# Normalising ahead of a gate, weight places read three chunks sooner, transposes one chunk later, in a vision tower with routed experts

## The reference, cut to what matters

```python
h = patch_embedding(x)                                  # 64 images, 37 tokens each, 256 wide
h = h + attention_0(layernorm(h))
x = layernorm(h)                                        # this stage holds the change
out = expert(x, sg, su, sd)                             # shared expert: silu(x sg') * (x su') sd', width 704
probs = softmax(x @ wr.T + rb)                          # 7 routed experts, the best 2 of each token
scores, idx = top_k(probs, 2); scores = scores / scores.sum(-1)
w = sum(scores[..., None] * one_hot(idx, 7), axis=-2)
h = h + out + sum(w[..., e] * expert(x, rg[e], ru[e], rd[e]) for e in range(7))
h = h + attention_1(layernorm(h))
h = h + gated_ffn_1(layernorm(h))
```

## Time and profile before

| | |
|---|---|
| median of 3 runs | 1051.48 us (1050.4 to 1051.73) |
| the profiled execution, its own time | 1051.63 us |
| its span, first to last instruction | 1049.8 us |
| mean granted clock of PE | 0.975 |
| shared expert with routing | 237 to 401 us of the span |
| routed experts | 401 to 712 us |
| busy: PE, DVE, ACT, POOL | 971.6, 709.0, 660.5, 359.1 us |

### The profile page before, as it was taken

How to read it: one execution, slowest core, us unless ns; L and a number is a source line. 1 busy time by engine, 2 the same in 40 slices (tenths; PEclk the granted TensorE clock), 3 DMA queues, 4 the chain that set the end, 5 groups by cost and what they waited for, 6 DMA issues and landing times.

```text
span 1049.8 us, 29183 instructions
## 1 busy us (share of the span) xinstructions
PE 971.6 (93%) x10745; PEld 892.2 (85%) x10746; DVE 709.0 (68%) x1393; ACT 660.5 (63%) x1206; POOL 359.1 (34%) x285
## 2 busy tenths in 40 slices
PE   4979999989999987999999999997899999799998
PEld 4967888868888886999999999996678888699998
DVE  3536677675556566899999999992566777655443
ACT  3337677855465635687777777772567678555652
POOL 0253454465665650111111111113545554611210
PEclk9999999989999998999999999999889999999999
DMA  6720000009211135111111111104311100000000
GB/s 231 240 96 3 2 3 3 3 7 357 41 35 31 40 75 221 35 36 40 35 35 40 40 35 35 40 30 141 81 26 26 26 3 4 2 13 12 24 25 24
DMA packets 30974, 57.67 MB, mean 55 GB/s; under 512 B 13202, under 2 KB 22418, under 8 KB 29724
## 3 DMA queue, kind: packets, MB, share of 16 engines
q1 hardware_dynamic: 15696, 38.38, 11.5%
q0 software_dynamic: 13664, 15.25, 4.8%
q10 hardware_dynamic: 1516, 2.65, 0.7%
HBM read 41.47 MB, written 14.67 MB: 53 GB/s over the span
## 4 chain that ended last, share of the span: by engine, by line
PE 72%; DVE 9%; ACT 9%; issue 5%; DMA 3%; POOL 1%; SPq 0%; DVEq 0%; ACTq 0%; POOLq 0%
PE ps L1400 19%; PE ps L1405 15%; PE ps L1407 14%; PE ps L1406 14%; PE ps L1805 3%; PE ps L1549 3%; PE ps L1538 2%; DVE Hd L1149 2%; DMA x_in<-in_xT_dram 2%; ACT L817 1%; ACT Hf_hi L811 1%; PE ps L1703 1%; ACT Sg L817 1%; DVE hsum L1139 1%; ACT L831 1%
## 5 line engine op out<-in xcount | busy, mean ns | idle before, releaser
L1303 DVE TENSOR_TENSOR tile_w<-arena,tile_w 128x704 fp32r<-128x704 f32 x129 | 142.7, 1134 | 26.9 <-ACT tile_w L880 24.2
L559 POOL DMA_INDIRECT routed_out<-yt,tile_to x43 | 42.1, 979 | 275.6 <-DVE yt L1321 271.5
L880 ACT ACTIVATE tile_w<-arena 128x704 fp32r x129 | 122.3, 984 | 1.4 <-issue 1.4
L1405 PE MATMUL ps<-tile_w,xTs 128*128 128x352 f32 x344 | 115.3, 335 | 4.5 <-DVE h L1276 3.0
L1406 PE MATMUL ps<-tile_w,xTs 128*128 128x352 f32 x344 | 111.6, 324 | 0.0
L1407 PE MATMUL ps<-tile_w,xTs 128*128 128x352 f32 x344 | 111.5, 324 | 0.0
L429 POOL TENSOR_TENSOR Km<-KT,cst 128x592 f32<-128x592 f32 x64 | 75.7, 1184 | 68.9 <-PE ps L1400 42.1
L1149 DVE TENSOR_TENSOR Hd<-Sg,ps 128x296 f32<-128x296 f32 x96 | 44.2, 461 | 81.2 <-ACT Sg L817 77.1
L811 ACT ACTIVATE Hf_hi<-Hd 128x296 fp32r<-128x296 f32 x96 | 43.3, 452 | 85.6 <-DVE Hd L1149 83.4
L1405 PE MATMUL ps<-xf_hi,gu_lo 128*128 128x296 f32 x272 | 85.8, 316 | 4.1 <-DVE Hd L1149 3.7
L1015 DVE SCALAR_TENSOR_TENSOR ps<-ps,bias 128x592 f32<-128x592 f32 x64 | 50.1, 782 | 53.0 <-PE ps L1400 53.0
(11 more groups left out here) (216 smaller groups left out, 3097.7 us busy)
## 6 DMA issues: line engine op xcount, KB each, us to landing
arena<-in_ew_dram SPq DMA_DIRECT2D x5, 2176.0 KB
x_in<-in_xT_dram SPq DMA_DIRECT2D x7, 888.0 KB, 5.4
xt<-routed_in SPq DMA_DIRECT2D x43, 129.0 KB, 2.0
arena<-in_ew_dram POOLq DMA_DIRECT2D x2, 2176.0 KB, 11.9
yg<-routed_out SPq DMA_DIRECT2D x8, 512.0 KB
out_dram<-h SPq DMA_DIRECT2D x8, 296.0 KB, 2.7
routed_in<-zero_x SPq DMA_DIRECT2D x12, 129.0 KB
qkv_w<-in_qkv_dram ACTq DMA_DIRECT2D x2, 768.0 KB, 6.2
```

What stands on the lines that cost most here:

```text
L880: act.activation(tile_w[half][0][:, cols], gate_up_of(w, half)[:, cols], ACT.Copy).then_inc(s.wh, 1)
L1303: dve.tensor_tensor(tile_w[half][1][:, cols], gate_up_of(w, half)[:, cols], tile_w[half][0][:, cols].bitcast(F32), ALU.subtract).then_inc( ...
L1405: pe.matmul(out_, w[1], x[0], start=start, stop=False)
```

## The change

Three things move; no work is added or taken away.

- In the routing, DVE's `norm` stood at `at` 4, after the gate and the rest of the hidden tile of that chunk, ahead of `slots_of`. Now it stands at the end of `at` 3, ahead of that gate.
- ACT and DVE read the first tile's place of weights in chunk 3 of the last group, with a wait for the table. Before, they read it after the whole shared expert. The waits for the transfers stay where they were.
- PE transposes the first tile's rows in chunk 4 of the last group instead of chunk 3, and ACT rounds them in chunk 5 instead of chunk 4.

```diff
@@ ACT, ffn: step
-                        if l == 0 and last and j == 4:
+                        if l == 0 and last and j == 3:
+                            act.wait_ge(s_table, 1)
+                            first_w.append(weights_of(act, 0))
+                            first_w.append(loads_of(act, 0))
+                        if l == 0 and last and j == 5:
                             upper_in(0, 0)
@@ ACT, routed
-                def upper_weights(t, w, half):
-                    if half == 0:
+                def upper_weights(t, w, half, ahead=True):
+                    if half == 0 and ahead:
                         act.wait_ge(s_exl, loads_of(act, t))
...
                 norms_idle(act)
                 rows_idle(act)
-                w = weights_of(act, 0)
-                upper_weights(0, w, 0)
+                w, loaded = first_w
+                act.wait_ge(s_exl, loaded)
+                upper_weights(0, w, 0, False)
                 upper_weights(0, w, 1)
@@ DVE, ffn: routing and step
                     if at == 4:
-                        if r + 1 < GROUPS:
-                            norm(r + 1)
                         slots_of(r, r % 2)
                     next(routes[r])
+                    if at == 3 and r + 1 < GROUPS:
+                        norm(r + 1)
...
+                        if l == 0 and last and j == 3:
+                            dve.wait_ge(s_table, 1)
+                            first_w.append(weights_of(dve, 0))
@@ DVE, routed
-                w = weights_of(dve, 0)
+                w = first_w[0]
                 lower_weights(0, w, 0)
@@ PE, ffn: step
-                        if l == 0 and last and j == 3:
+                        if l == 0 and last and j == 4:
                             pe.wait_ge(s.r, RCHAIN * GROUPS)
                             tile_in(0, 0, 0)
```

More of the change, by code:

```diff
@@ L610, in _ @@
             act.preload_act_table_set("natural_log_exp_and_others")
+            first_w = []
             def upper_patches(g, b, loaded):
@@ L926, in _ @@
             routing = F[0]
-            first_routes = []
+            first_routes, first_w = [], []
             R = slice(0, W2)
```

## The result

The changed kernel took 1044.07 us (median of 17 runs, 1041.13 to 1050.7). The kernel before took 1051.48 us in the 17 runs beside it (1045.6 to 1058.47). The ratio is 0.9935, interval 0.9916 to 0.9955: between 0.45 and 0.84% faster. The forecast was 1048.7, so the direction was right, and the forecast gain was less than half of what came.

The account below looks back on a forecast made before the run. PE is busy most of the span, so changes on other engines pay only where PE idles for them. Terms 1.35 + 0.8 + 0.79 + 0 = 2.94 us off 1051.63 gave 1048.7 us; range 1046.0 to 1050.9.

Parts of the forecast that it names:

- PE falls to 1.2 GHz more often: Rival: longer or shifted PE waits at 417 and in the routing bring more slow stretches; 1054.1 us, chance 0.06.
- the forecast's own range: Whole kernel: 1047.5 to 1049.9 us around the forecast of 1048.7, which had chance 0.53.
- Term 1: Routing, PE's logits: start 0.27 us sooner in five rounds, 0.15 us behind ACT's copy of rows; 1.35 us.
- Term 2: Routing, DVE from `xn` to the next gate: three of six rounds shrink by half of 0.5 us more; 0.8 us.
- DVE paces every round: Rival, routing: each of six rounds gives its whole 0.77 us, 5.4 in all; 1046.2 us, chance 0.12.
- Term 3: End of the shared expert: the first tile's transposes, one chunk later, find their rows landed; 0.79 us.
- Term 4: Passage to the routed experts: weight places read early; 0.9 us turns into a longer wait for tile 2's rows; 0 us.
- Only the passage pays: Rival, routing: logits start sooner but idle a little later; gain only 0.79 us, 1050.8 us, chance 0.20.
- Tile 2's rows land with their issue: Rival, routed experts: row packets are served between the weights, PE keeps 0.9 us more; 1047.8 us, chance 0.09.

Follow-up runs that it names:

- norm_only: The kernel before with only DVE's `norm` moved ahead of the gate, table reads and transposes as before: 1045.51 us, ratio 0.9950.
- passage_only: The changed kernel with the move of `norm` undone, so only the transposes and the reads of the weight place are moved: 1050.19 us, ratio 0.9985.
- the fitted pair: The kernel before and the changed kernel, each with unneeded PE matmuls only in rounds where PE waits ahead of the logits: 1046.09 and 1043.85 us.
- pad_old_place: The changed kernel with two unneeded DVE multiplications (0.75 us) per round where `norm` stood before: 1050.40 us, ratio 0.9987.
- pad_in_wait: The changed kernel with two unneeded DVE multiplications (0.75 us) per round ahead of `norm`, in DVE's wait for `rsd`: 1046.90 us, ratio 0.9961.
- late_load: The changed kernel with POOL's load of the last two experts' weights held behind a wait for tile 2's rows: 1050.86 us, ratio 0.9986.
- warm: The changed kernel with two unneeded PE matmuls ahead of the logits of each round, in the wait for ACT's copy: 1045.91 us, ratio 0.9941.

## Why the prediction fell short, point by point

**The step that failed.** The sum had four terms and none for the clock. The text let the clock move only in the rival "PE falls to 1.2 GHz more often", and in the forecast's own range as "part of a stretch at 1.2 GHz more or less". I had the fact in hand, a stretch at that level behind a wait and its price of 1.8 us a round, and used it only against the change. A change that shortens PE's waits in six rounds had to be credited with it. The sizes: a straight line through before's 84 runs falls by 0.9 us per 0.001 of clock, and the clock rose by 0.0037, some 3.4 us. Read at an equal clock of 0.979, the lines through the runs stand at 1048.3 for before and 1045.6 for after, 2.8 us for the edits alone, close to the 2.94 that I gave. Read the same way, norm_only stands at 1045.7 and passage_only at 1048.2.

By the traces the edits are worth more: 3.4 us over the rounds at a like clock (0.43, 0.35, 0.45, 0.74, 0.62 and 0.86, from the table, the stretches matched with passage_only and norm_only), and with the passage's 1.5 about 4.9. The medians differ by 7.4 and the means by 6.8 (1051.78 and 1044.99), so 4.9 leaves 1.9 for the clock and 2.8 leaves 4.0. The fillers don't decide it: with the waits filled in both, the change gave 0.9939 - 0.9914 = 0.25%, 2.6 us, for the fitted pair and 0.9954 - 0.9941 = 0.13%, 1.4 us, for the other, with an uncertainty of 3 to 4 us each. That edits and clock share the gain is shown; the split between 2.8 and 4.9 for the edits stays open.

**Term 1, the logits start sooner, 1.35.** Right in mechanism, mis-sized: 2.1 us, from 6.3 to 4.2 in the groups. Five times some 0.4 and not 0.27 (round 2's wait from 2.08 to 1.71, later ones from 1.11 to 0.67 and from 0.94 to 0.50), in good part since I carried the 0.15 us from behind DVE's `xn` over to ACT's copy, where it is 0.06: with 0.06, round 2 gives 279.04 - 278.68 = 0.36. The 0.07 more in the other four is not taken apart.

**Term 2, the DVE chain behind it, 0.8.** Mis-sized: 3.4 - 2.1 = 1.3 us in the rounds, and 0.33 more in the last group: from the logits of group 7 to the product ahead of the transposes it is 392.90 - 353.75 = 39.15 us in before and 387.77 - 348.95 = 38.82 in norm_only. I took half of 0.5 in three rounds; rounds 4, 5 and 6 gave 0.3, 0.6 and 0.4 beyond term 1. That it was three is luck: I chose the rounds at full clock, in before 1, 4 and 6 of the table, but round 1 gave nothing beyond term 1 and round 5, with its stretch at 1.2 GHz, did. What tells them apart is whether DVE paces, and not the clock. The rounds of pad_old_place and pad_in_wait show it to be DVE's place and not its load. The rival "DVE paces every round" is wrong for rounds 1 to 3.

**Term 3, 0.79.** The length was right to 0.01, yet it is not a term beside the others: norm_only lost the same wait without it (0.14 us from the product to the transposes, against 0.93 in before).

**Term 4, 0.** The first routed product came 1.0 us sooner, and tile 2's wait took 0.5 of that back. Between norm_only and after, which have a stretch at 1.2 GHz at the same place, tile 2's transposes moved by 0.3 us from the logits of group 7 (411.70 - 348.95 = 62.75, and 62.48). So the part was worth a little more than the 0 that I gave. The landing was tied to POOL's load: it came 16.84 us behind POOL's issue in before (417.72 - 400.88) and 16.50 in after (411.12 - 394.62), and late_load confirmed that.

**"Only the passage pays"** had 0.20 and is refuted by norm_only. **"Slower: PE falls to 1.2 GHz more often"** had the sign of the clock reversed. **"Tile 2's rows land with their issue"** did not come, by late_load, though the queues do take turns.

## What to carry to other kernels

Where PE's granted clock is below 1 in the very rounds that a change touches, write a term for the clock with both signs: a wait shortened there pays its length and a part of a stretch at 1.2 GHz, here between 0.4 and 1.4 times as much again. The test is cheap: fill the wait with matmuls that nobody needs, and see over several runs what the clock gives back before touching the chain. Two edits that shorten what the same transfer hides behind are not to be added.

## What the runs showed of the hardware

In the kernel before, PE waits 0.9 to 2.1 us once in a round of some 18 us of otherwise dense matmuls, and in its trace three of six rounds held a stretch at 1.2 GHz. Filling 0.85 us or more of each wait raised the mean clock of the kernel from 0.976 to 0.983, filling half of that to 0.979. The Trainium skill (TensorE: Matmul & The Clock Gate, A second HAM failure mode: psum-queue depth-cycling) tells of short idle times between groups of matmuls that make the clock go to and fro; this case agrees, with 0.95 over six rounds against 1.00 with the waits filled.

The wait ahead of the logits is not the whole of it. In the changed kernel's round 6 PE falls to 1.2 GHz behind logits that waited for nothing; its idle time, 0.77 us, stood just ahead, for DVE's `h`. At 331.59 a product of 296 columns takes 0.45 us instead of 0.30:

```profile
328.95 0.38 PE L1415 MATMUL ps<-Hf_hi,dn_lo 128*128 128x296 f32 x1 [0.77 <-DVE h L1286]
...
329.84 1.17 PE L1410 MATMUL ps<-r_w,xn 128*74 128x7 f32 x16
...
331.59 0.45 PE L1416 MATMUL ps<-xf_lo,gu_hi 128*128 128x296 f32 x1
```

pad_old_place, too, has the changed kernel's short waits ahead of the logits and yet a clock of 0.976. Its DVE pad brings back idle time of PE elsewhere in the round. Round 4, in before, after and pad_old_place, the first figures being its length and PE's busy time:

```profile
298.94:317.05 18.11, 16.95 (x126) 15.54 (x127) 11.14 (x39) 10.23 (x18) 11.31 (x10) 1.00 0.17 34
294.67:312.04 17.37, 16.79 (x127) 15.58 (x127) 11.23 (x39) 10.11 (x19) 11.65 (x10) 1.00 0.18 33
300.36:318.41 18.05, 16.98 (x126) 15.55 (x127) 11.90 (x41) 10.11 (x19) 11.67 (x10) 1.00 0.17 32
```

PE is idle 1.16, 0.58 and 1.07 us of it, and the mean clocks of the three kernels are 0.9758, 0.9795 and 0.9764. So the clock goes with PE's idle time in the round, wherever it lies. That is read off these kernels and was not tested by itself, and warm, above, does not fit it well; what else counts stays open.
